# An RWKV layer and a selected/window/latent attention layer on one core: selected scores as a product of their own with the keys stationary, another order of the projections, and eight PSUM banks for the last stage

## What is computed

```python
nq = _rms(x @ w_cq, g_qnorm)                       # 96 latent channels of the queries
q = concat([nq @ w_dq_nope, rope(nq @ w_dq_rope)]) # 16 heads, 32 + 64 channels
ckv = _rms(x @ w_ckv, g_kvnorm)                    # 32 latent channels
k1, v1 = concat([ckv @ w_dk_nope, rope(x @ w_krope) / 16]), ckv @ w_dv
sel = take(x, sort(top_k(x @ w_imp, 32)))          # 32 selected tokens of each batch
ks, vs = rope(sel @ w_selk), sel @ w_selv
kw, vw = rope(x @ w_wink), x @ w_winv
a1 = _attn(q, k1, v1, causal=True)                 # latent keys
a2 = _attn(q, ks, vs, causal=False)                # selected keys, 32 columns
a3 = _attn(q, kw, vw, causal=True)                 # window keys
out = (g0 * a1 + g1 * a2 + g2 * a3) @ w_proj
# then, after the norm, over the 8 batches:
c = sigmoid(x @ wf.T + c @ uf.T + bf) * c + sigmoid(x @ wi.T + c @ ui.T + bi) * tanh(x @ wc.T + c @ uc.T + bc)
h = tanh(x @ wo.T + c_final @ uo.T + bo)           # for all batches, with the last cell
```

## Time and profile before

| | us |
|---|---|
| median of 3 runs | 1965.31 (1965.22 to 1974.73) |
| the profiled execution | 1968.04 |
| its span, first to last instruction | 1966.3 |
| layer 0 and preparation, to the first score | 235.2 |
| the 32 groups, first score to the last `op` | 1681 |
| the end | 50 |

### The profile page before, as it was taken

The page is one execution under the profiler, slowest core; times in us unless marked ns, Lnnn a source line. Parts: engine busy times, 40 slices in busy tenths (PEclk is TensorE's granted clock), DMA queues, the critical chain, the costliest instruction groups (busy, mean ns, idle before and its releaser), DMA issues.

```text
span 1966.3 us, 34441 instructions
## 1 busy us (share of the span) xinstructions
PE 1795.2 (91%) x10716; PEld 1072.5 (55%) x10716; DVE 1265.1 (64%) x3791; ACT 1171.8 (60%) x3575; POOL 676.7 (34%) x697
## 2 busy tenths in 40 slices
PE   5666699999999999999999999999999999999995
PEld 3333455555556555555565555655555556555552
DVE  5999576666665666666666666565666666666672
ACT  3564366656666666666666666566666666666651
POOL 0565523433334323332343333333333233333300
PEclk8787799999999999999999999999999999999998
DMA  4001111121111111111112111121111111211101
GB/s 161 1 0 27 26 49 39 38 54 49 32 45 32 51 30 45 38 39 49 39 39 53 49 39 38 41 55 24 39 40 40 45 39 41 51 49 38 39 1 43
DMA packets 71298, 80.94 MB, mean 41 GB/s; under 512 B 29520, under 2 KB 37840, under 8 KB 70992
## 3 DMA queue, kind: packets, MB, share of 16 engines
...
## 4 chain that ended last, share of the span: by engine, by line
PE 63%; DVE 15%; issue 7%; POOL 7%; ACT 5%; SPq 1%; DMA 0%; DVEq 0%; POOLq 0%; ACTq 0%
PE bank L1856 21%; PE bank L1883 12%; PE bank L1816 8%; PE bank L1709 3%; PE bank L1708 2%; PE bank L1766 2%; PE bank L1704 2%; PE bank L1779 1%; PE bank L1762 1%; DVE arena L1432 1%; DVE arena L1244 1%; DVE arena L1455 1%; PE bank L1827 1%; ACT arena L1017 1%; PE bank L1787 1%
## 5 line engine op out<-in xcount | busy, mean ns | idle before, releaser
L1455 DVE CUSTOM_DVE_ANT_0 arena<-bank,W 128x512 f32<-128x512 f32 (+3 forms) x1024 | 480.0, 487 | 521.4 <-PE bank L1856 355.5
L1017 ACT ACTIVATE arena<-arena 128x512 f32<-128x512 f32 (+3 forms) x1024 | 570.2, 559 | 362.0 <-DVE arena L1455 358.6
L1856 PE MATMUL bank<-arena 96*128 96x512 f32 (+6 forms) x2048 | 713.8, 450 | 0.0
L1856 PEld LDWEIGHTS bank<-arena 96*128 96x128 f32 x2048 | 349.9, 191 | 172.4 <-issue 135.4
L1883 PE MATMUL bank<-W,arena 128*128 128x128 f32 x2560 | 428.6, 281 | 0.1
L1883 PEld LDWEIGHTS bank<-W,arena 128*128 128x128 f32 x2560 | 301.0, 143 | 220.8 <-issue 173.7
L1466 DVE COPY arena<-bank 128x512 f32<-128x512 f32 (+1 forms) x512 | 318.4, 622 | 73.3 <-PE bank L1883 70.2
L734 POOL TENSOR_TENSOR arena<-arena,one 128x512 f32<-128x512 f32 x64 | 66.6, 1041 | 799.9 <-DVE arena L1423 612.2
L1816 PE MATMUL bank<-arena 128*32 128x256 f32 (+1 forms) x3072 | 219.6, 358 | 1.0 <-DVE arena L1466 0.7
L1017 ACT ACTIVATION_READ_ACCUMULATOR arena<-arena 128x1 f32 x1024 | 197.1, 192 | 0.0
L996 ACT ACTIVATE arena<-bank 128x384 f32<-128x384 f32 x256 | 124.5, 486 | 91.9 <-PE bank L1883 90.1
...
## 6 DMA issues: line engine op xcount, KB each, us to landing
...
```

Of the source, the lines that this page charges most:

```text
L1017: done = A(here, here, ACT.Exp, bias=nmax[:, c:c + 1], scale=-1.0, accum_out=lsum[:, c:c + 1])
L1455: last = v.tensor_tensor_reduce(Pb[:, s % 4, at_p:at_p + n], bank[turn.score_bank(s)][:, at + lo:at + lo + n], w("mask", T - n), -1.0, 3e3 ...
L1856: last = MM(B_[:, at:at + lo + n], query(t), Kb[a][g % 2][0:QD, h, skip:skip + lo + n], start=True, stop=True)
```

## The change

Selected scores: `Kb[0]` holds only the latent keys, and the score products of the latent half have 384, 256 and 128 columns. A new task `s2` in the shared bank multiplies the selected keys, 32 columns of each head stationary, with the queries of all 512 tokens, into the 32 partitions of each head. DVE reads it with a transpose of 32x32 blocks into `p2` (step 10 + 1, or 9 + 1 in q = 1), shifts at step 12 instead of 13, ACT exponentiates at 13, and after the scaling at step 16 DVE turns the blocks back into `p2T` at step 17 (`selected_turned`, four instructions). ACT's copies of the selected columns and keys and the task `p2T` with its read are gone. A score product waits for the maximum of three units before in all cases.

Order: `group_tasks` has other steps for the projections, nk3 before x1k. `MOVER` gives tile 3 to ACT. SP lays the shared key, queries and latent queries of q = 3 before the selected keys, which wait for the `s2` of q = 2. The four parts of `rt` are placed 6 elements or 32 elements away from the former multiples of 512.

End: the gates have banks 0 to 2 and the halves of their products that use the cell before are made ahead; the outputs of the eight batches have a bank each, the product with the tokens is made ahead, and the three stages run two batches apart, written out instead of in a loop.

```diff
-def laid(a, tiles):
+def laid(tiles):
     at, out = 0, []
     for t in reversed(tiles):
-        lo = scores_at(a, t)
-        out.append((t, (t + 1) * P, lo, at))
-        at += lo + (t + 1) * P + (lo if t == 0 else 0)
+        out.append((t, (t + 1) * P, at))
+        at += (t + 1) * P
...
-MOVER = {3: "dve", 2: "act", 1: "dve"}
+MOVER = {3: "act", 2: "act", 1: "dve"}
 PROJ = ["x1q", "x2q", "nq", "x1k", "x2k", "nk3", "nk1", "vw", "vl"]
-READER = {"op": "dve", "ks": "dve", "o2": "dve", "rank": "dve", "score": "dve", "gates": "dve"}
+READER = {"op": "dve", "s2": "dve", "ks": "dve", "o2": "dve", "rank": "dve", "score": "dve", "gates": "dve"}
...
-    steps, proj, extra = {"op": 8, "p2T": 18, "o2": 20}, (0, 2, 4, 6, 7, 9, 11, 13, 15), []
+    steps, proj, extra = {"op": 8, "s2": 10, "o2": 20}, (0, 1, 3, 6, 7, 5, 11, 13, 15), []
     if g == 0:
-        steps, proj = {"op": 7, "p2T": 18, "o2": 20}, (0, 1, 3, 5, 6, 9, 10, 21, 22)
+        steps, proj = {"op": 7, "s2": 10, "o2": 20}, (0, 1, 3, 6, 8, 5, 9, 21, 22)
         extra = [(7, "z3T"), (11, "score"), (12, "vs"), (13, "gates"), (21, "rank")] if first else [(12, "z4T"), (14, "gf"), (15, "gi"), (19, "gc")]
     if first:
-        proj = (0, 1, 3, 5, 6, 9, 10, 14, 16)
+        proj = (0, 1, 3, 6, 8, 5, 9, 14, 16)
     if g == 2 and not last:
-        proj = (0, 1, 3, 5, 6, 9, 10, 11, 12)
+        steps["s2"], proj = 9, (0, 1, 3, 6, 7, 5, 10, 11, 12)
         extra = [(15, "cqkv"), (17, "kr"), (19, "sel"), (21, "ks"), (22, "nqT")]
     if g == 3 and not last:
-        proj = (1, 2, 4, 6, 7, 10, 11, 13, 15)
+        proj = (1, 2, 4, 6, 7, 5, 11, 13, 15)
         extra = [(22, "vs")]
-    out = [(steps["p2T"], "p2T", q), (steps["o2"], "o2", q)]
+    out = [(steps["s2"], "s2", q), (steps["o2"], "o2", q)]
...
+        rt = [cv(T), cv(T + RT_PAD)[:, RT_PAD:], cv(T + 32 - RT_PAD)[:, 0:T], cv(T + RT_PAD)[:, RT_PAD:]]
+        cv(32 - RT_PAD)
+        Qb, Kb, V = [cv(HG, T)], [[cv(HG, T)], [cv(HG, T)]], [[cv(NT, HG * VH)], [cv(NT, HG * VH)]]
...
+                lay_shared(i + 1)
+                lay_queries(turn, 3)
+                lay_latent_queries(turn, 3)
                 sp.wait_ge(s_ksd, i + 2)
+                sp.wait_ge(s_g, turn.filled("s2", 2))
                 lay_selected()
-                lay_shared(i + 1)
-                lay_group(turn, 3)
+                lay_keys(turn, 3)
+                lay_latent_keys(turn, 3)
                 lay_group(turn, 4, shared=i + 1)
...
-                        if turn.g(q) == 1 and s % GU == 1:
-
-                            act.wait_ge(s_c, turn.b + 1)
-                        done, at_p = None, 0
-                        for t, n, lo, at in laid(a, tiles):
-                            if lo:
-
-                                picked = slice(0, NT, NT - 1) if t == 0 else slice(t, t + 1)
-                                m = 2 if t == 0 else 1
-                                scores = B_[:, at:at + m * (KEEP + P)].rearrange("p (m x) -> p m x", m=m)[:, :, 0:KEEP]
-                                made = A(p2h[:, h, picked], scores, ACT.Copy)
-                                if h == HG - 1 and t == 0:
-                                    made.then_inc(s_s2, 1)
-                        for t, n, lo, at in laid(a, tiles):
+                        at_p = 0
+                        for t, n, _ in laid(tiles):
...
+                elif name == "s2":
+                    v.transpose(p2, G[:]).then_inc(s_gd, 1)
...
+                def selected_turned(q):
+                    v.wait_ge(s_p2n, p0 + (q + 1))
+                    if q > 0:
+                        v.wait_ge(s_g, turn.filled("o2", q - 1))
+                    elif not turn.first:
+                        v.wait_ge(s_g, turn.filled0)
+                    for t in range(NT):
+                        last = v.transpose(p2T[:, (NT - 1 - t) * P:(NT - t) * P], p2[:, t * P:(t + 1) * P])
+                    last.then_inc(s_p2t, 1)
...
-                    if at == 13:
+                    if at == 12:
                         selected_shifted(q)
+                    if at == 14:
+                        selected_sums(q)
                     if at == 15:
-                        selected_sums(q)
+                        selected_inverse()
                     if at == 16:
-                        selected_inverse()
+                        selected_normed(q)
                     if at == 17:
-                        selected_normed(q)
+                        selected_turned(q)
...
+            def out_gated(b):
+                v.wait_ge(s_ho, b + 1)
+                if b >= 4:
+                    v.wait_ge(s_oT, b - 3)
+                TS(hg[:, b % 4], ho[:, b % 4], modc[:, 11, b:b + 1], None, ALU.mult).then_inc(s_hg, 1)
+
+            def out_added(b):
+                v.wait_ge(s_oT, b + 1)
+                TT(ob[:, b].rearrange("p j c -> p (j c)"), X[:, b * T:(b + 1) * T], bank[out_bank[b]][:], ALU.add).then_inc(s_ob, 1)
+
+            for b in range(B + 2):
+                if b < B:
+                    out_gated(b)
+                if b >= 2:
+                    out_added(b - 2)
...
-                    pe.wait_ge(s_p2n, p + 1)
-                    for t in range(NT):
-                        last = pe.transpose(G[:, (NT - 1 - t) * P:(NT - t) * P], p2[:, t * P:(t + 1) * P], ident)
+                elif name == "s2":
+                    if g == 0:
+                        pe.wait_ge(s_ksm, turn.nb * (16 * 3 * HG) + 16 * 3 * HG)
+                    for j in range(HG):
+                        last = MM(G[j * KEEP:(j + 1) * KEEP], KS[0:QD, g, j], Qb[g % 2][0:QD, j], start=True, stop=True)
                 elif name == "o2":
+                    pe.wait_ge(s_p2t, p + 1)
...
-                            pe.wait_ge(s_p if scores_at(a3, tiles3[0]) else s_max, u0 + (before + 1))
+                            pe.wait_ge(s_max, u0 + (before + 1))
...
-                            skip = 0 if lo or a else KEEP
-                            last = MM(B_[:, at:at + lo + n], query(t), Kb[a][g % 2][0:QD, h, skip:skip + lo + n],
-                                      start=True, stop=True)
-                            if lo and t == 0:
-
-                                at += lo + n
-                                last = MM(B_[:, at:at + KEEP], query(NT - 1), Kb[0][g % 2][0:QD, h, 0:KEEP],
-                                          start=True, stop=True)
+                        for t, n, at in laid(tiles):
+                            last = MM(B_[:, at:at + n], query(t), Kb[a][g % 2][0:QD, h, 0:n], start=True, stop=True)
...
+            def gate_past(n, name):
+                MM(bank[n][:], w(f"u{name}T"), c_st, start=True, stop=False)
+
+            def gate_now(n, name):
+                MM(bank[n][:], w(f"w{name}T"), HT[:, (B - 1) * T:], start=False, stop=True).then_inc(s_tg, 1)
+
+            def out_first(b):
+                MM(bank[out_bank[b]][:], w("wo2T"), HT[:, b * T:(b + 1) * T], start=True, stop=False)
+
+            def out_cell(b):
+                MM(bank[out_bank[b]][:], w("uoT"), c_st, start=False, stop=True).then_inc(s_op, 1)
+
+            def out_turned(b):
+                pe.wait_ge(s_hg, b + 1)
+                for j in range(NT):
+                    last = pe.transpose(bank[out_bank[b]][:, j * P:(j + 1) * P], hg[:, b % 4, j * P:(j + 1) * P], ident)
+                last.then_inc(s_oT, 1)
+
+            all_units, all_rows = B * NG * GU, B * NG * GR
+            pe.wait_ge(s_p, all_units)
+            pe.wait_ge(s_c, B)
+            gate_past(0, "f")
+            gate_past(1, "i")
+            fill(last_turn, "op", NG - 2)
+            gate_past(2, "c")
+            out_first(0)
+            out_first(1)
+            pe.wait_ge(s_nrm, all_rows)
+            out_first(2)
+            pe.wait_ge(s_iv, all_rows)
+            out_first(3)
+            fill(last_turn, "z4T", 0)
+            pe.wait_ge(s_ga, last_turn.read("z4T"))
+            for n, name in enumerate(("f", "i", "c")):
+                gate_now(n, name)
+            out_first(4)
+            for n in range(3):
+                pe.wait_ge(s_tga, n + 1)
+                out_first(5 + n)
             pe.wait_ge(s_c, B + 1)
-            with pe.Fori(0, B // 2) as i:
-                for e in range(2):
-                    MM(bank[e][:], w("wo2T"), HT[:, ds((i * 2 + e) * T, T)], start=True, stop=False)
-                    MM(bank[e][:], w("uoT"), c_st, start=False, stop=True).then_inc(s_op, 1)
-                for e in range(2):
-                    pe.wait_ge(s_hg, i * 2 + e + 1)
-                    for j in range(NT):
-                        last = pe.transpose(bank[2 + e][:, j * P:(j + 1) * P], hg[:, e, j * P:(j + 1) * P], ident)
-                    last.then_inc(s_oT, 1)
+            for b in range(B + 2):
+                if b < B:
+                    out_cell(b)
+                if b >= 2:
+                    out_turned(b - 2)
```

114 lines of the change are left out of this document (48 added, 66 removed).

## The result

The changed kernel takes **1946.1 us** (median of 4 runs, 1943.62 to 1950.73) against 1968.65 for the kernel before on the same chip: a ratio of **0.9886, interval 0.9864 to 0.9907**, 22 us less. The forecast was 45 less. Its profiled execution took 1946.7 us, span 1944.9, against 1968.0 and 1966.3: 21 us less. The range held the time; the change in it was overestimated by a factor of two.

The account below looks back on a forecast made before the run. PE, busy 95 to 97% of each group, was taken as the bound, plus its few waits. Loop -30, end -22 and clock +7 made -45 us, from the median 1965.3 to 1920 us; range 1875 to 1950.

Parts of the forecast that it names:

- scores and s2: On PE in each group: narrower score products -1.4 us, the new selected-score product +1.0 us (ends 0.9 and 3.4).
- x2k: PE's stall at this key projection for ACT's read of x1k should go: -0.6, -1.2, -0.6, -1.5 us in a batch's four groups.
- nk1's DMA wait, g0: First group of a batch: PE stalls about 3 us before the selected-score product, behind nk1's late read; +2.8 us (0 to 3.2).
- steps 12 to 14: Selected scores' reduction and shift, a step earlier on DVE, delay a move PE needs: +1.3, +0.3, +0.4, +0.3 us by group.
- steps 16 to 20: PE's turning and its wait go, but a 1.1 us wait for unit 18 comes: -1.8, -0.2, -1.3, -0.2 us by group.
- the end: After the loop, from z4T's read: gates half done ahead, outputs every 1.35 us instead of 2.98; -22 us (-18 to -24).
- the clock: Half of eight waits in the batches' first groups bring a 1.2 GHz dip of about 1.7 us each: +7 us.
- the rival in which narrow products run one after another: The selected-score product in each group takes 3.4 us instead of 1.0: +77 us, 1997 us; chance 0.05.
- The first rival, in which the DMA wait is hidden: In each batch's first group the DMA wait is hidden and DVE catches up: 1884 us, or 1865; chance 0.27.
- Movers: ACT takes the 256 moves of 512 columns, +1.4 us busy a group; no charge to the time.
- the rival on ACT: ACT becomes the bound in the tall steps, 0.3 us longer per pair: +60 us, about 1955 us; chance 0.13.

Follow-up runs that it names:

- The experiment on g3's queries: Changed kernel with x1q, x2q and nq in each batch's fourth group filled at steps 0, 1, 3 instead of 1, 2, 4; ratio to the kernel before 0.9915.

## Why the prediction was wrong

**The sum.** Groups at full clock went from 54.78, 49.02, 56.10 and 49.57 us to 56.15, 48.11, 54.63 and 49.39; of g0 that is the one with the shortest wait. By its own terms, us a batch, measured from the starts of the steps in the two traces, to some 0.2 us:

| term | forecast | measured |
|---|---|---|
| scores and s2 | -1.6 | about 0 |
| x2k | -3.9 (-0.6, -1.2, -0.6, -1.5) | -2.0 (-0.6, -0.9, -0.3, -0.2) |
| nk1's DMA wait, g0 | +2.8 | +2.8 |
| steps 12 to 14 | +2.3 (1.3, 0.3, 0.4, 0.3) | +2.4 (1.0, 0.6, 0.2, 0.6) |
| steps 16 to 20 | -3.5 (-1.8, -0.2, -1.3, -0.2) | -4.3 (-1.8, -0.6, -1.3, -0.6) |
| batch | -3.9 | -1.2 |

Seven batches make 19 of the 24 us that the sum misses against the profiled execution; the first and the last groups make 2, the end 1.5, the clock and longer waits 1, the start 0.6. The 2.7 us a batch are two terms that were too large, x2k by 1.9 and scores with s2 by 1.6, less 0.8 that steps 16 to 20 gave back.

**x2k, above all in g3, is the step that failed.** In g3 it forecast -1.5 us and got -0.2. I took -1.5 from the one batch that I had looked into. There PE stood 1.60 us; in five of the seven g3, and in every g1, it was 0.94. PE's timeline before the change, in the g1 of the same batch:

```profile
943.82 1.12 PE L1709 MATMUL bank<-arena,W 128*128 128x512 f32 x2 [0.94 <-ACT arena L924]
```
And I let all of it go. Two waits stand in the changed kernel's g3. PE's timeline, and ACT's:

```profile
1046.70 1.12 PE L1716 MATMUL bank<-arena,W 128*128 128x512 f32 x2 [0.20 <-ACT arena L929]
...
1051.25 1.12 PE L1716 MATMUL bank<-arena,W 128*128 128x512 f32 x2 [0.29 <-ACT arena L926]
...
1046.05 0.60 ACT L929 ACTIVATE arena<-bank 128x512 f32<-128x512 f32 x1
```
The first is new: the change puts nk3 at step 5, one step behind nq, and PE waits for ACT's read of nq (L929), which stands behind a move and an exponential. By the starts of the steps it costs 0.4 to 0.5 us. The second is what is left of the old wait at x2k, some 0.25 us: in g3 the change leaves x1q at step 1, so the rotation of the queries starts a step later than in g1. The experiment on g3's queries takes both away together. I had written "starts at steps 6 and 7" of all groups, where g0 has 6 and 8, and had not looked at what g3's own list does to the start of the chain and to nk3.

**Scores and s2: two sizes, too large and too small.** A low unit lost 0.14 to 0.25 us and a tall one of 416 columns 0.05: about -1.1 a group, not -1.4. I had compared unlike rows: the 0.99 us of the earlier trace rows is followed by value products, the 0.66 of the earlier trace rows by a turning. Like for like it is 0.99 to 0.85 and 0.90 to 0.66. s2 is 1.00 us from its start to the next score; the changed kernel's PE in g1:

```profile
951.65 0.55 PE L1883 MATMUL bank<-W,arena 128*128 128x128 f32 x3
952.12 1.06 PE L1779 MATMUL bank<-arena 96*32 96x512 f32 x8
953.12 0.92 PE L1862 MATMUL bank<-arena 96*128 96x256 f32 x4
```
The value products side by side were the right row, and the rival in which narrow products run one after another is refuted. The turning ahead of it is some 0.1 longer: about +1.1. The Trainium skill, "TensorEngine Tiling (Array Packing)", Key Properties, says that a change of tiling mode drains the engine; that 0.1 us is all that the trace leaves for it here, by the difference of two spacings.

**Steps 12 to 14: right in the sum, by luck.** g0 and g2 were overestimated and g1 and g3 underestimated by as much. Reduction and shift cost 1.73 us, not 1.4: the subtraction grew by 0.4 beside POOL's multiplication. The Trainium skill, "SBUF — State Buffer", Who interferes with whom, says that a Vector instruction with two SBUF inputs contends with a GpSimd instruction that reads SBUF. The trace agrees: two inputs in SBUF, 0.69 us alone and 1.09 beside it. I had priced a moved instruction by where it stood before, and not looked at who is beside it where it goes.

**Steps 16 to 20: the mechanism right, its size too large.** PE does wait for unit 18's exponential, behind the transposes. I had 1.1 us of wait; by the starts of the steps it is 0.5 at step 20 (0.29 of it idle in the profile) and 0.3 at step 19, together 0.8. And what went, the wait and the turning, was 1.4 and not 1.25. DVE's chain was 3.1 us, not 3.5: the maximum of unit 17, with 384 columns, takes 0.48 and not 0.6, the transposes 0.81 and not 1.0, and the maximum of unit 18 0.58 and not 0.7.

**nk1's wait in g0: right in place and size**, 2.45 us in a usual g0. What the prediction did not see is that it covered a second wait, from its own edit of the keys' steps, on POOL. The first rival, in which the DMA wait is hidden, would not have come to 1884 by that alone: with the wait taken away it was 1942.

**Movers: "no charge" was right, but they had no gain of their own in the sum either.** Giving them back costs 27 us. The prediction counted DVE's relief only in steps 16 to 20, and there not by itself.

**Clock: +7 came out, from other parts.** Half of the g0 waits were to bring a stretch at the lower level, at 1.7 us each. Six of seven did, but at 1.2 us each: g0 took 1.24 to 2.18 us more than at full clock, and what is above 1.2 is the wait itself, longer than 1.93. What the groups take above their length at full clock is 10 us before and 18 after. The lower clock is about 8 of the one and 15 of the other: 7 in g0 and 7.5 in five of the seven g2, where it was 6 in three of them before. The Trainium skill's section on oscillation ("TensorE: Matmul & The Clock Gate", "HAM oscillation — how this bites in real kernels") has the engine start again throttled after each DMA wait. In number the trace is nearer to that than to half; in us it is half. Such stretches are in one to five of the seven g2 in every kernel, the one before too; what decides there stays open.

**The end: -20.5 of -22**, as worked out, the output period 1.30 us.

**Two sums that don't come out.** For the rival on ACT, 0.3 us on 8 pairs in 32 groups is 77 us and not 60, and the way from there down to 1955 is worked out from no row. In the end, 26.8 less 12 is 14.8 and not 14.6. The first is no part of the forecast, and the second touches it by 0.2 us.

**Luck.** The time fell into the range because the range reached up to the rival on ACT, which did not come. The forecast change was twice the measured one, and no rival stood for what happened: the loop's gains and its new waits cancelled.
